# First routing pass moved ahead of the expert stage, unit tables built in eight parts, in a two-layer transformer kernel with a top-2 mixture of experts

## What is computed

```python
x = x + attn0(layernorm(x)); x = x + swiglu_int(layernorm(x))
x = x + causal_attn(layernorm(x))            # 16 heads of 8, layernorm on q and k
z = layernorm(x)                             # the routed feed-forward, LOOPS = 2
for _ in range(2):
    zn = rmsnorm(z) * norm_w
    scores = softmax(zn @ router_w)          # 8 experts
    vals, idx = top_k(scores, 2); vals /= sum(vals) + 1e-9
    z = z + sum_e cw[:, e] * (silu(zn @ w1[e]) * (zn @ w3[e])) @ w2[e]
x = x + z
```

## Time and profile before

| | |
|---|---|
| median of 3 runs | 2308.6 us (2305.61 to 2311.1) |
| the profiled execution's own time | 2307.91 us |
| its span | 2306.2 us |
| mean granted TensorE clock | 0.959 of full |
| `experts` begins at | 1551 us of the span |
| busy over the span | PE 87%, DVE 80%, ACT 63%, POOL 53% |
| indirect DMAs on POOL | 512, of 0.98 us each (busy), issued 1.27 us apart |

### The profile page before, as it was taken

How to read it: one execution, slowest core, us unless ns; L and a number is a source line. 1 busy time by engine, 2 the same in 40 slices (tenths; PEclk the granted TensorE clock), 3 DMA queues, 4 the chain that set the end, 5 groups by cost and what they waited for, 6 DMA issues and landing times. The chain is left out here.

```text
span 2306.2 us, 47356 instructions
## 1 busy us (share of the span) xinstructions
PE 2011.8 (87%) x14679; PEld 982.9 (43%) x14679; DVE 1844.3 (80%) x5277; ACT 1462.1 (63%) x3354; POOL 1232.1 (53%) x1710
## 2 busy tenths in 40 slices
PE   5999999999988999899999999974888988988991
PEld 1222222222222465444444444432555766766661
DVE  8999999999999576888888888847777676676555
ACT  1788888888888332677777777751545655655550
POOL 6343343343321021676767676634476777667776
PEclk9999999999999999899999999985999999999996
DMA  7355344344341001434232433302233443433453
GB/s 183 102 130 139 102 130 139 102 129 139 102 129 48 1 19 37 100 70 101 69 99 71 96 74 93 76 26 74 87 106 101 122 117 114 118 108 113 130 139 99
DMA packets 224610, 226.94 MB, mean 98 GB/s; under 512 B 34032, under 2 KB 187504, under 8 KB 224368
## 3 DMA queue, kind: packets, MB, share of 16 engines
q1 hardware_dynamic: 152432, 164.62, 27.0%
q0 software_dynamic: 16384, 33.59, 5.0%
q10 hardware_dynamic: 55552, 25.71, 3.9%
HBM read 96.48 MB, written 125.76 MB: 96 GB/s over the span
## 5 line engine op out<-in xcount | busy, mean ns | idle before, releaser
L702 ACT ACTIVATE mid_PT<-mid_ps 128x512 f32<-128x512 f32 (+2 forms) x1792 | 914.0, 568 | 258.4 <-PE mid_ps L583 250.5
L785 DVE TENSOR_REDUCE mid_nmax<-mid_ps 128x1 f32<-128x512 f32 (+2 forms) x1280 | 776.4, 657 | 61.5 <-PE mid_ps L562 36.4
L562 PE MATMUL mid_ps<-KT,QT 48*128 48x512 bf16 (+3 forms) x2048 | 604.5, 351 | 68.3 <-DVE mid_nmax L785 49.6
L583 PE MATMUL mid_ps<-QT,KT 64*128 64x512 bf16 (+3 forms) x2048 | 562.5, 346 | 2.5 <-ACT mid_PT L702 2.2
L599 PE MATMUL mid_ps<-mid_PT,vv 128*32 128x512 f32 (+3 forms) x4096 | 465.1, 527 | 16.3 <-POOL mid_PT L914 12.5
L562 PEld LDWEIGHTS mid_ps<-KT,QT 48*128 48x128 bf16 x2048 | 158.9, 94 | 585.2 <-DVE mid_nmax L785 397.4
L782 DVE CUSTOM_DVE_ANT_0 mid_PT<-mid_ps,mask 128x512 bf16<-128x512 f32 (+1 forms) x512 | 304.5, 619 | 68.8 <-PE mid_ps L562 64.0
L1395 PE MATMUL moe_ps<-moe_w,moe_xinT 128*128 x638 | 341.5, 618 | 0.0
L1506 POOL DMA_INDIRECT rows_in<-moe_xn,moe_scat_idx x256 | 250.2, 977 | 161.9 <-DVE moe_scat_idx L1696 86.0
L1519 POOL DMA_INDIRECT moe_yg<-rows_out,moe_gat_idx x256 | 250.8, 980 | 80.6 <-issue 77.2
L1450 ACT ACTIVATE moe_xinT<-moe_ps,norm_w 128x128 f32<-128x128 f32 x319 | 116.7, 366 | 275.8 <-PE moe_ps L1407 186.9
(11 more groups left out here) (266 smaller groups left out, 3060.0 us busy)
## 6 DMA issues: line engine op xcount, KB each, us to landing
l_spread<-mid_slots SPq DMA_DIRECT2D x128, 384.0 KB, 5.4
rows_in<-mid_blank SPq DMA_DIRECT2D x64, 512.0 KB, 3.8
QT<-l_spread SPq DMA_DIRECT2D x128, 192.0 KB, 4.3
KT<-l_spread SPq DMA_DIRECT2D x128, 192.0 KB, 5.2
moe_xin<-rows_in SPq DMA_DIRECT2D x319, 64.0 KB
rows_out<-moe_y ACTq DMA_DIRECT2D x319, 64.0 KB
x<-in_L_attn_x_dram SPq DMA_DIRECT2D x8, 512.0 KB, 6.6
QT<-mid_mrows SPq DMA_DIRECT2D x256, 6.0 KB
```

The costliest lines, as they stand in the source:

```text
L562: mm = pe.matmul(ps[:, bank, n_keys * a:n_keys * (a + 1)], QT[rows, par, pair, i * P:(i + 1) * P], KT[rows, par, pair, 0:n_keys], start=Tr ...
L583: mm = pe.matmul(ps[:, bank, m * a:m * (a + 1)], KT[rows, own, pair, i * P:(i + 1) * P], QT[rows, own, pair, SEQ - m:SEQ], start=True, sto ...
L702: act.activation(weights_of(r, i, heads), ps[:, ring(S2, n - 2, k), 0:widths[i] * len(heads)], ACT.Exp, scale=scale).then_inc(exp_done, 1)
L785: dve.tensor_reduce(to, of, X_AXIS, ALU.max, negate=True).then_inc(s1_used, 1)
```

## The change

1. A new class `Lead` holds pass 0. Its PE, ACT, DVE and POOL parts are called from the causal attention in slots of steps 64 to 67 (`off` 0 to 3). Its scratch lies in the unused end of the array that held the attention weights; `z` and `xn` of the pass share their place with two arrays of the integer feed-forward. The three first of the 16 scatters of pass 0 (`SENT = 3`) stand in POOL's step 67, between the two last additions to `x`; the other 13 come first in `experts`.
2. `experts` begins with the tables of unit 0 on DVE, then pass 1, then tile 0. `EARLY` covers pass 1 alone, and `transfers` lacks `s0`.
3. SP issues the loads of the expert weights at the end of `middle`, after the last weighted sum (`av_done`).
4. `make_tables` is cut into 8 parts, which stand as stages 20 to 27 of the pass that ends the unit, in the same table `begin`. SP waits for a new semaphore `rows_made`, raised after part 5; gathers still wait for `tables`, raised after the last part.
5. `region`, `falling`, `upper` and `ones` are made in `middle`; two iotas and two casts fall away.

```diff
@@ new
+class Lead:
+    ZT, SCRATCH, SENT = 14464, 15488, 3
...
+    def tensor(self, pe, off, u, s1_used, s1_total):
+        if (off, u) in ((1, 5), (1, 7)):
+            a = (u - 5) // 2
+            if a == 0:
+                pe.wait_ge(s1_used, s1_total)
+                pe.wait_ge(self.z_ready, 1)
+            for t in range(4):
+                mm = pe.transpose(self.psT[a][:, t * P:(t + 1) * P], self.z[:, 4 * a + t, :], self.w["ident"][:, :])
+            mm.then_inc(self.t_made, 1)
+        if (off, u) == (1, 14):
+            pe.wait_ge(self.t_used, 2)
+            for t in range(IT):
+                mm = pe.matmul(self.psR[:, t, :], self.zT[:, t * P:(t + 1) * P], self.w["router"][:, :], start=True, stop=True)
+            mm.then_inc(self.r_made, 1)
+        if (off, u) == (2, 15):
+            pe.wait_ge(self.const, 2)
+            pe.wait_ge(self.sel_ready, 1)
+            selb = self.m["selb"]
+            pe.matmul(self.psK, self.upper[:, :], selb, start=True, stop=False)
+            for t in range(IT):
+                mm = pe.matmul(self.psK[:, t + 1:, :], self.ones[:, :],
+                               selb[:, t, :].unsqueeze(1).to_broadcast([P, IT - t, EXPERTS]), start=False, stop=(t == IT - 1))
+            mm.then_inc(self.k_made, 1)
+    def scalar(self, act, off, u):
+        m = self.m
+        if (off, u) in ((1, 8), (1, 11)):
+            a = (u - 8) // 3
+            act.wait_ge(self.t_made, a + 1)
+            act.activation(self.zT[:, 4 * P * a:4 * P * (a + 1)], self.psT[a], ACT.Copy, scale=self.w["norm_w"][:, 0:1])\
+               .then_inc(self.t_used, 1)
+        if (off, u) == (2, 8):
+            act.wait_ge(self.shifted, 1)
+            act.activation(m["pr"], m["sh"], ACT.Exp).then_inc(self.exp_ready, 1)
+            act.wait_ge(self.second_ready, 1)
+            act.activation(m["e2"], m["second"], ACT.Exp).then_inc(self.e2_ready, 1)
+    def vector(self, dve, off, u, x_added):
...
+        if (off, u) == (0, 0):
...
+            dve.tensor_tensor(self.z[:, :, :], self.z[:, :, :], each_row(rstd), ALU.mult).then_inc(self.z_ready, 1)
...
+            dve.tensor_tensor(self.xn[:, :, :], self.z[:, :, :], each_row(rstd), ALU.mult).then_inc(self.xn_ready, 1)
+        if (off, u) == (1, 15):
+            c = self.linked
+            dve.wait_ge(self.r_made, 1)
...
+        if (off, u) == (2, 15):
+            c = self.linked
+            dve.wait_ge(self.k_made, 1)
...
+            dve.tensor_copy(self.scat[:, :, :], self.at[:, :, :]).then_inc(self.scat_ready, 1)
+        if (off, u) == (3, 15):
...
+    def scatter(self, pool, i):
+        if i == 0:
+            pool.wait_ge(self.zeroed, 16 * STEPS)
+            pool.wait_ge(self.xn_ready, 1)
+            pool.wait_ge(self.scat_ready, 1)
+        a, t = divmod(i, IT)
+        pool.indirect_dma_start(self.rows_in[0], bass.IndirectOffsetOnAxis(ap=self.scat[:, a, t:t + 1], axis=0),
+                                self.xn[:, t, :], None).then_inc(self.scattered[0], 16)
@@ attention (step of pe; the same for act with lead_pass.scalar and dve with lead_pass.vector)
+                    if lead_pass:
+                        lead_pass.tensor(pe, n - STEPS, u, s1_used, SLOTS * STEPS)
@@ attention, gpsimd
+                if lead_pass and n == STEPS + 3:
+                    for i in range(lead_pass.SENT):
+                        lead_pass.scatter(pool, i)
@@ middle, sync
             sp.wait_ge(zeroed, 16 * STEPS)
+            sp.wait_ge(second.signals["av_done"], STEPS)
+            load_experts(sp)
@@ experts
-    STAGES = 20
+    STAGES, TABLES = 20, 8
-    transfers = ("s0 s1 s2 s3 g8 s4 s5 g9 ...
+    transfers = ("s1 s2 s3 g8 s4 s5 g9 ...
-        return [(k, s) for k, at in begin.items() for s in range(STAGES) if at + s * length(k) // STAGES == n]
+        return [(k, s) for k, at in begin.items() for s in range(STAGES + TABLES) if at + s * length(k) // STAGES == n]
@@ run
-            for k in range(EARLY):
-                for s in range(STAGES):
+            for k in range(1, EARLY):
+                for s in range(STAGES + TABLES):
                     side(k, s)
@@ sync
-            sp.dma_start(w13[:, :, 0:FF], ...
...
-                    sp.wait_ge(tables, u + 1)
+                    sp.wait_ge(rows_made, u + 1)
@@ gpsimd
+            for i in range(lead.SENT, 2 * IT):
+                lead.scatter(pool, i)
@@ vector, side
-                    if k + 1 == first_of[unit_of[k]] + sizes[unit_of[k]]:
-                        make_tables(unit_of[k])
+                if s >= STAGES and k + 1 == first_of[unit_of[k]] + sizes[unit_of[k]]:
+                    make_tables(unit_of[k], s - STAGES)
@@ make_tables: the same instructions, under
+                if part == 0: full, ntiles, memset of run_sum
+                if part == 1: pair, base, move, last_t
+                if part == 2: passed, shares
+                if part == 3: before, expert
+                if part == 4: before, live, row
+                if part == 5: row_of, coded, weighted, sums, words  (raises rows_made)
+                if 6 <= part < 6 + n_it: moved, moved_by, gat_idx of one pass  (the last raises tables)
+            for part in range(TABLES):
+                make_tables(0, part)
             run(tile, side, 0)
```

More of the change, by code:

```diff
@@ L1166, in _, with experts @@
             pool.memset(blank[:, :], 0.0).then_inc(blanked, 1)
+            lead_pass.opens(pool)
             first.gpsimd(pool, range(-7, STEPS + 4))
             second.gpsimd(pool, range(-8, STEPS + 8))
-def experts(nc, x, z, w, tri, ins, out, rows_in):
-    IT = 8
-    GROUPS = BATCHES * TILES // IT
+def experts(nc, x, z, w13, w2, w_in, out_done, lead, w, tri, ins, out, rows_in):
     CHUNKS = 4
@@ L1197, in experts @@
              16: 270, 17: 283, 18: 292, 19: 314, 20: 325}
-    transfers = ("s0 s1 s2 s3 g8 s4 s5 g9 s6 g10 s7 g11 s8 g12 s9 g13 s10 g14 s11 s12 g15 s13 g16 s14 g17 g18 s15 "
+    transfers = ("s1 s2 s3 g8 s4 s5 g9 s6 g10 s7 g11 s8 g12 s9 g13 s10 g14 s11 s12 g15 s13 g16 s14 g17 g18 s15 "
                  "g19 g20 g21 g22 g23").split()
@@ L1530, in _ @@
         def _(dve):
-            dve.wait_ge(const, 2)
+            c = Chain(dve, lead.chain, lead.linked.n)
+            dve.wait_ge(lead.const, 3)
             dve.tensor_copy(iota_f[:, :], iota_i[:, :])
-            dve.tensor_copy(region[:, :], reg_i[:, :])
-            dve.tensor_copy(falling[:, :], fall_i[:, :])
             dve.memset(selb[:, IT, :], 0.0)
@@ L1657, in side @@
                         dve.wait_ge(xn_ready, k + 1)
[L1659 removed]
+                sel = sel_of(k)
                 if s == 9:
@@ L1705, in make_tables @@
                 full_u, passed_u, shares_u = full[:, :, 0:ht], passed[:, 0:n_tiles, :], shares[:, 0:n_tiles, :]
+                expert, before, live, row = (tab[:, a, 0:n_tiles] for a in range(4))
                 def per(t, n, k=P):
                     return t.unsqueeze(1).to_broadcast([k, n, EXPERTS])
-                c.link(dve.tensor_scalar(full_u, iota_f[:, 0:ht].unsqueeze(1).to_broadcast([P, EXPERTS, ht]),
-                                         float(P), None, ALU.mult))
-                c.link(dve.tensor_tensor(full_u, count.unsqueeze(2).to_broadcast([P, EXPERTS, ht]), full_u, ALU.is_gt))
@@ L1720, in make_tables @@
-                c.link(dve.tensor_tensor(shares_u, passed_u, per(ntiles[0:1, :], n_tiles, 1), ALU.mult))
-                expert, before, live, row = (tab[:, a, 0:n_tiles] for a in range(4))
-                dve.tensor_reduce(before, shares_u, X_AXIS, ALU.add)
-                c.link(dve.tensor_reduce(expert, passed_u, X_AXIS, ALU.add))
-                c.link(dve.tensor_tensor(before, iota_f[0:1, 0:n_tiles], before, ALU.subtract))
-                dve.tensor_scalar(before, before, float(P), None, ALU.mult)
@@ new lines, in make_tables @@
+                if part == 3:
+                    dve.tensor_reduce(before, shares_u, X_AXIS, ALU.add)
+                    c.link(dve.tensor_reduce(expert, passed_u, X_AXIS, ALU.add))
+                if part == 4:
+                    c.link(dve.tensor_tensor(before, iota_f[0:1, 0:n_tiles], before, ALU.subtract))
+                    dve.tensor_scalar(before, before, float(P), None, ALU.mult)
+                    dve.tensor_scalar(live, expert, EXPERTS - 0.5, None, ALU.is_lt)
+                    c.link(dve.tensor_scalar(row, expert, float(CAP), None, ALU.mult))
+                    c.link(dve.tensor_tensor(row, row, before, ALU.add))
@@ new lines, in make_tables @@
+                if part == 5:
+                    own = slice(base_of[u], base_of[u] + n_tiles)
+                    dve.tensor_tensor(row_of[0:1, own], row, live, ALU.mult)
+                    code = coded[:, :, :].rearrange("o c i -> o (c i)")[:, 0:n_tiles]
+                    c.link(dve.tensor_tensor(code, expert, live, ALU.mult))
+                    c.link(dve.tensor_tensor(weighted[:, 0:n_words, :], coded[:, 0:n_words, :], places[:, 0:n_words, :], ALU.mult))
```

(3 more changed lines are left out.)

282 lines of the change are left out of this document (193 added, 89 removed).

## The result

The changed kernel takes 2282.1 us (median of 4 runs, 2281.31 to 2285.29); the kernel before, beside it, 2309.61 (4 runs, 2305.61 to 2311.1). The ratio is 0.9886, 95% interval 0.9869 to 0.9903: 27.5 us or 1.1% faster. The forecast was 2266, 16 us less. The profiled execution took 2285.29 us, the slowest of its four; its span of 2283.5 us stands against 2306.2: 22.7 us less.

What follows compares the result with a forecast made beforehand. Row tiles were taken to set the end until POOL has no idle time. POOL's transfer s13 39.7 us earlier, plus 1.75 of POOL's waiting, gave 41.4: span 2306.2 to 2264.8, with 1.7 around it 2266 us; range 2255 to 2289.

Steps and rivals of the forecast that it cites:

- What sets the end: Experts' stage: the end moves exactly as the row tiles move, until POOL has no idle time left.
- The lead-out grows by 5.0: Attention's end, up to the last addition to `x`: pass 0's transposes 2.2, router 1.8, DVE's slots and counts 1 us.
- The seam, less 0.6 for POOL's constants: Between attention and `experts`: DVE starts some 0.6 us sooner, as POOL's constants are made earlier; an estimate.
- 0 and stays 0: Moving the weight loads from the stage's start to the attention's last step costs 0, since nobody waited for them.
- Tile 0 18.7 earlier: Start of the row tiles: 17.7 us from pass 1 starting sooner, plus 0.98 that PE waited for `xin`.
- Tile 23 19.1 earlier: Unit 1's first tile, held until POOL's transfer s2 lands: at 1636.4 against 1655.54.
- The pieces: Tables in eight parts of 0.90 us among the tiles: saves 5.7 at pass 4, 2.4 at 6, 4.5 each at 8, 10, 12.
- rival 5: PE's idle spells beside the pieces bring the half clock for all eight tiles: 24 us slower, 2332 us; chance 4%.
- rivals 1 and 2: First: pieces wholly hidden, 48.1 us, 2259.8, chance 15%. Second: pieces pay nothing, 18.7 us, 2289, chance 13%.
- Sum: Gains added along POOL's transfers: s5 24.8, s12 35.2, s13 39.7 us earlier, and 41.4 us at the end.
- Rival 3: Pass 0's hops are waited for in order, the attention's end slips by 24 us, only pieces count: 2285 us; chance 6%.
- rival 2: Pieces pay nothing, only the lead-in counts: 18.7 us, 2289 us; chance 13%.

Runs made afterwards that it cites:

- `control`: The changed kernel itself, run again beside the follow-up kernels on a chip like the first: 2282.2 us, ratio 0.9884 to the kernel before.
- `pieces`: The kernel before with only the tables cut into eight pieces and SP waiting for `rows_made`: 2287.6 us, ratio 0.9918 to the kernel before.
- `late`: The changed kernel with PE's part of pass 0 in PE's waits behind the last weighted sum, no scatter in the attention: 2271.9 us, ratio 0.9849.
- `late_z`: `late`, with DVE also waiting for step 62's masks before it makes z: 2268.8 us, ratio 0.9832 to the kernel before.
- `burst2`: The changed kernel with the tables made in one piece again, pass 0 still in the lead-out: 2300.3 us, ratio 0.9968 to the kernel before.
- `loads_seam2`: The changed kernel with the weight loads back at the start of `experts`, on a chip like the first: 2280.0 us, ratio 0.9874.
- `router_last`: The changed kernel with pass 0's router products, DVE's choice and counts behind the last projection, no scatter in the attention: 2280.7 us, ratio 0.9889.

## Why the forecast was right in kind and 16 us off

- **What sets the end: right.** From s13's start to the end of the span it is 239.8 us before, 238.1 in the changed kernel, 236.7 in `control` and `pieces`, 237.2 in `late`, 236.8 in `late_z`; `burst2`, which keeps a wait before g21 (1.72), has 239.8. Every gain of the tiles up to s13 came out at the end. POOL's idle time left up to s5 is 44.9 (12.4 + 8.2 + 16.6 + 7.7), where 43 was said.
- **The lead-out grows by 5.0, bounds 0 to 6.8: the step that failed.** It grew by 11.8 by its own measure, outside the bounds. They priced PE's work and held the clock of the rest fixed. The clock was full from 1536 in the earlier trace rows; but just ahead of that, near the place of the transposes, the trace of before has 0.50 from 1530 to 1534, with PE busy all the time. With the transposes it stayed at 0.50 until past 1552, so the router took 3.58 and not 1.8, the last weighted sum 3.21 and not 1.71. Work of 5.8 us at the half clock cost some 10.6; the 1 us for DVE's slots came as said, with 1.2.
- **The seam, less 0.6 for POOL's constants: failed.** The weight loads "0 and stays 0" were 0 alone, but 3.2 to 4.1 us (`control`, changed kernel) with three scatters beside them, whose packets they held up. I had asked who waits for them, not what passes the seam at the same time.
- **Tile 0 18.7 earlier:** 7.4 in the profiled run, 9.6 in `control`. `late`, with a lead-out that grew by 2.2, has 19.1, so the rest of the chain was sound.
- **Tile 23 19.1 earlier, held by s2:** 5.2 (7.3 in `control`). Between tiles 4 and 9 another 3 to 4 us go: tile 0 no longer waits for its rows, and so PE runs into DVE, which is only 6.3 us earlier (8.5 in `control`) with pass 2's z. PE waits 1.75 and 2.23 us there, and the half clock is back from 1604 to 1607. This shows in `burst2` and `loads_seam2` too, and not in `pieces` or `router_last`.
- **The pieces: right in mechanism, sized a quarter too high.** Forecast 5.7, 2.4, 4.5, 4.5, 4.5, in all 21.6 for passes 4 to 12; in the changed kernel 5.1, 0.5, 3.0, 4.2, 3.3, in all 16.1; alone 16.3. Beside pass 10 the tiles 160 to 166 take 14.9 us instead of 9.8, 5.1 too much where 4.0 was said. From 1784 to 2230 the clock is 1.00 throughout, so rival 5 fell, as did rivals 1 and 2. Pass 6 missed most of all, and there rival 5 has a small part: behind waits of PE of 2.38 and 1.90 us (1770 and 1778) the changed kernel is at the half clock for some 3.4 us each time; beside pass 4 it is there from 1706 to 1710, behind a wait of 3.08 (in `control` the wait is 3.05 and the clock stays full). The forecast counted on the full clock for all of them. The passage of the Trainium skill that stands behind rival 5 ("TensorE: Matmul & The Clock Gate", A second HAM failure mode) does not fit the waits of 0.5 to 0.85 us beside pass 10.
- **Sum.** At s13 39.7 was forecast and 21.0 came: 13.9 are missing at tile 23, 0.4 between tiles 23 and 42 and 5.5 in the pieces, less the 1.0 that tile 179 was to lose to s10. Behind s13 1.7 came as forecast (3.1 in `control`). Rival 3, a lead-out that slips by 24, named the place of the loss, and its sign, the last addition to `x` 10 us late or more, came; its mechanism, hops waited for in order, did not. 12.4 + 4.1 = 16.5 us came.
- **The range was met partly by luck.** 2282 lies nearer to rival 3 (2285) and rival 2 (2289) than to the forecast. The bounds of the lead-out (+5, -2) do not cover 11.8 and 4.1; the range does, because it reached up to rival 2, pieces that pay nothing, and that did not happen. The time alone would not have told these apart; the traces do.

## What to carry to other kernels

Before work is put "into a hole", look at which clock PE has there and what it does to the work behind it: pass 0's transposes, router and slots lengthened the lead-out by 11.8 us in front of the last weighted sum and by 2.2 behind it. A bound on added PE work has to include the work that is there already, at the half clock. And a step that nobody waited for should be checked against everything that the change puts beside it: the loads and the scatters were nearly free one at a time, and together cost 3 to 4 us.
